# Node blocks in a turned order, a bank cleared and closed by one column, shorter bounds, and an eviction moved amid index copies

## The reference

```python
edge_index = stack([src, dst])
x = _layernorm(x + L0(x, node_type, edge_index, edge_type, ...))   # 3 relational convolutions, 5 relations
x = _layernorm(x + L1(x, ..., edge_index))                          # attention, edge score exp(-leaky_relu(s1[src] + s2[dst]))
x = _layernorm(x + L2(x, edge_index, edge_weight, ...))             # segment_sum(edge_weight * x[src], dst) @ W.T + b
x = _layernorm(x + L3(x, edge_index, edge_attr, ...))               # mean of edge_attr over dst, then a small MLP
```

## Time and profile before

| | before |
|---|---|
| median of 3 runs | 5267.58 us (5249.11 to 5267.61) |
| the profiled execution | 5260.04 us, span 5258.3 us |
| busy: PE, PEld | 3666.9 us (70%), 2929.5 us (56%) |
| busy: DVE, POOL, ACT | 2687.7 us (51%), 2380.1 us (45%), 1162.6 us (22%) |
| gathers of the three passes, line 608 | 2160, mean 1029 ns |
| visits (line 1130), blocks evicted (line 693) | 434, 385 |
| mean granted TensorE clock | 0.823 of full speed |
| chain that ended last | PE 36%, issue 20%, POOL 14%, DMA 13%, DVE 9% |

### The profile page before, as it was taken

How to read it: one execution, slowest core, us unless ns; L and a number is a source line. 1 busy time by engine, 2 the same in 40 slices (tenths; PEclk the granted TensorE clock), 3 DMA queues, 4 the chain that set the end, 5 groups by cost and what they waited for, 6 DMA issues and landing times.

```text
span 5258.3 us, 105311 instructions
## 1 busy us (share of the span) xinstructions
PE 3666.9 (70%) x20468; PEld 2929.5 (56%) x20688; DVE 2687.7 (51%) x6973; ACT 1162.6 (22%) x3868; POOL 2380.1 (45%) x2346
## 2 busy tenths in 40 slices
PE   4777566666777777766767677677777777584872
PEld 1233455555666666555555555566566666574862
DVE  7654344444444444355555555455554554794336
ACT  0122111111111122122222222223322322351112
POOL 0000233344455555466666666566666665002530
PEclk8999777787888888877777778788888888797986
DMA  2022222222333444322323233344444444255740
GB/s 75 33 63 68 73 61 67 74 73 81 97 101 115 121 120 123 108 76 78 86 80 84 81 90 89 105 115 117 126 124 123 129 125 115 104 208 150 203 133 13
DMA packets 478385, 526.90 MB, mean 100 GB/s; under 512 B 96596, under 2 KB 398238, under 8 KB 474670
## 3 DMA queue, kind: packets, MB, share of 16 engines
q1 hardware_dynamic: 252780, 246.52, 15.1%
q0 software_dynamic: 85824, 199.51, 14.0%
q10 hardware_dynamic: 139746, 80.46, 5.2%
HBM read 399.82 MB, written 126.39 MB: 100 GB/s over the span
## 4 chain that ended last, share of the span: by engine, by line
PE 36%; issue 20%; POOL 14%; DMA 13%; DVE 9%; DVEq 3%; ACT 2%; ACTq 1%; SPq 1%; POOLq 0%; another core or an unknown queue 0%
POOL msg_r L608 14%; DMA msg_r<-y_tab,idx_r 9%; PE psum L1566 9%; PE psum L1636 4%; PE psum L1568 2%; DMA msg_r<-x_tab,idx_r 2%; DVE shot_r L1136 2%; PE psum L1747 2%; PE psum L1709 1%; PE psum L1432 1%; PE psum L1494 1%; DVE h_t L1365 1%; PE psum L1748 1%; PE psum L1524 1%; PE psum L1506 1%
## 5 line engine op out<-in xcount | busy, mean ns | idle before, releaser
L608 POOL DMA_INDIRECT msg_r<-y_tab,idx_r x2160 | 2221.9, 1029 | 2223.9 <-issue 1161.6
L1566 PE MATMUL psum<-shot_r 128*128 128x200 f32 x2604 | 1000.1, 486 | 465.1 <-DVE shot_r L1136 437.3
L1130 DVE SCALAR_TENSOR_TENSOR shot_r<-edge_f,win_base,iota 128x600 bf16<-128x600 f32 x434 | 366.4, 844 | 1197.1 <-PE psum L1568 740.7
L684 ACT COPY idx_r<-row_i 128x1 int32 x2142 | 395.6, 190 | 2246.6 <-DMA msg_r<-y_tab,idx_r 2044.3
L1566 PEld LDWEIGHTS psum<-shot_r 128*128 128x128 f32 x2604 | 554.8, 262 | 476.5 <-issue 472.1
L1115 DVE TENSOR_SCALAR hot_r<-iota,edge_g 128x128 f32<-128x128 f32 x1602 | 454.4, 357 | 186.4 <-PE psum L1748 148.8
L1568 PEld LDWEIGHTS psum<-shot_r 128*100 128x100 bf16 x2604 | 444.7, 171 | 115.0
L1568 PE MATMUL psum<-shot_r 128*100 128x128 bf16 x2604 | 462.3, 271 | 0.0
L1747 PE MATMUL psum<-msg_r,shot_r 128*128 128x128 f32 x1440 | 338.1, 321 | 175.3 <-DMA msg_r<-y_tab,idx_r 94.6
L1636 PEld LDWEIGHTS psum<-hot_r,msg_r 128*128 128x128 f32 x2880 | 408.9, 218 | 16.7 <-DMA msg_r<-y_tab,idx_r 6.8
L1636 PE MATMUL psum<-hot_r,msg_r 128*128 128x128 f32 x2880 | 405.8, 300 | 11.3 <-DMA msg_r<-y_tab,idx_r 4.5
(11 more groups left out here) (322 smaller groups left out, 4932.6 us busy)
## 6 DMA issues: line engine op xcount, KB each, us to landing
msg_r<-in_attr SPq DMA_DIRECT2D x882, 64.0 KB
h_t<-count_tab SPq DMA_DIRECT2D x25, 1600.0 KB, 6.6
w_tab<-shot_r ACTq DMA_DIRECT2D x385, 100.0 KB
count_tab<-shot_r ACTq DMA_DIRECT2D x385, 100.0 KB
h_t<-w_tab SPq DMA_DIRECT2D x24, 1600.0 KB, 8.0
msg_r<-y_tab,idx_r POOLq DMA_INDIRECT x2160, 2.6
xn<-heavy_tab SPq DMA_DIRECT2D x76, 320.0 KB
y_tab<-y_s SPq DMA_DIRECT2D x25, 640.0 KB, 2.9
```

The source lines that it names most:

```text
L608: pool.indirect_dma_start(out=msg_r[:, q, 0:width], out_offset=None, in_=table, in_offset=bass.IndirectOffsetOnAxis(ap=idx_r[:, q:q + 1], ...
L684: nc.scalar.copy(idx_r[:, q:q + 1], of[:, q:q + COLS - U + 1][:, bass.ds(c0, 1)]).then_inc(s_idx[k], 1)
L1130: V.scalar_tensor_tensor(out=key_b, in0=of(KEY, KW), scalar=win_base[:, bass.ds(w, 1)], in1=to(KW), op0=ALU.subtract, op1=ALU.is_equal).th ...
L1566: T.matmul(win_ps, low_f[:, i, :], weighted_f[:, i, :], start=False, stop=False)
```

## The change

It has five parts.

1. **Turned order.** Position s of the running order now stands for block (s + 264) % 384 (`window_at`). `win_first` and `win_n`, from which `win_tab` is made, are copied from PSUM in two parts each so that they lie in that order. `win_base` and the rows of `w_tab` and `count_tab` go by the block's own number.
2. **One column.** `clear` and `close` of the block's bank write column 240 alone instead of 512 columns. Column 240 belongs to neither part.
3. **Bounds.** `window_of` takes a minimum and a maximum instead of remainders and quotients. `win_tab`'s second number is how many visits a block has.
4. **`window_at`** adds a remainder on VectorE and on ScalarE.
5. **Eviction amid the copies.** `one_group` calls `window_out_of_psum` behind the third `next_row` instead of the sixth.

```diff
+TURNED, SPARE = 264, 240
         def window_of(eng, x):
-            x = bounded(eng.snap((x + (AHEAD_OF - 1)) % AHEAD_OF), 0, PAST * NW, "it counts groups of the passes")
-            past = eng.snap((x // NW + (PAST - 1)) // PAST)
-            over = bounded(eng.snap((x + (AHEAD_OF - (NW - 1))) % AHEAD_OF * past), 0, PAST * NW, "it is how far x lies past the last window")
-            return x, over, bounded(eng.snap(x - over), 0, NW - 1, "the last window comes again where x is past it")
+            x = bounded(eng.snap(x - 1), 0, PAST * NW, "it counts groups of the passes")
+            slot = eng.alloc_register(name=f"slot{next(numbers)}")
+            eng.reg_alu(slot, x, NW - 1, op=ALU.min)
+            slot = eng.snap(slot, min_val=0, max_val=NW - 1)
+            over = eng.alloc_register(name=f"over{next(numbers)}")
+            eng.reg_alu(over, x, NW - 1, op=ALU.max)
+            over = eng.snap(over, min_val=NW - 1, max_val=PAST * NW)
+            return x, bounded(eng.snap(over - (NW - 1)), 0, PAST * NW, "it is at least the last window"), slot
...
-            at, over, w = x
-            v0, v1, c0, n_last = loaded(eng, win_tab[0:1, bass.ds(w, 1), :].rearrange("a b c -> a (b c)"),
-                                        most=(MOST, MOST, CHUNKS, CHUNKS))
-            return eng.snap(v0 + over * n_last), eng.snap(v1 + over * n_last), c0
+            at, over, slot = x
+            v0, n, c0, last = loaded(eng, win_tab[0:1, bass.ds(slot, 1), :].rearrange("a b c -> a (b c)"),
+                                     most=(MOST, CHUNKS, CHUNKS, CHUNKS))
+            v0 = eng.snap(v0 + over * last)
+            return v0, eng.snap(v0 + n), c0
+
+        def window_at(eng, slot):
+
+            return bounded(eng.snap((slot + TURNED) % NW), 0, NW - 1, "it is a remainder")
...
             def window_out_of_psum(x):
-                n, _, w = x
+                n, w = x[0], window_at(act, x[2])
...
                         next_row(k, of, c0, before16, q)
-                window_out_of_psum(x)
+                    if q == UH - 1:
+                        window_out_of_psum(x)
...
-            V.tensor_copy(win_first, psum[0:1, 4, 0:NW])
-            then(V.tensor_copy(win_n, psum[0:1, 5, 0:NW]))
+            for to, bank in ((win_first, 4), (win_n, 5)):
+                V.tensor_copy(to[:, 0:NW - TURNED], psum[0:1, bank, TURNED:NW])
+                last = V.tensor_copy(to[:, NW - TURNED:NW], psum[0:1, bank, 0:TURNED])
+            then(last)
...
-            V.tensor_scalar(out=win_tab[:, :, 1], in0=visited, scalar1=1.0, scalar2=None, op0=ALU.add)
+            V.tensor_copy(win_tab[:, :, 1], win_n)
...
             def window_hots(x):
-                w = x[2]
+                w = window_at(dve, x[2])
...
-                clear(psum[:, 2, :])
+                clear(psum[:, 2, SPARE:SPARE + 1])
...
-                close(psum[:, 2, :], s_wsum)
+                close(psum[:, 2, SPARE:SPARE + 1], s_wsum)
```

## The result

The changed kernel takes 5116.35 us, median of 4 runs (5114.44 to 5138.07), where the kernel before took 5258.34 in the same comparison (5244.24 to 5267.61). The ratio is 0.974, 95% interval [0.970, 0.978]: 142 us less, where 305 were forecast. The profiled execution has a span of 5112.8 us against 5258.3, and a mean granted clock of 0.823, as before.

What follows compares the result with a forecast made beforehand. No engine was taken as the bound but loops between engines: VectorE against TensorE in pass 0, through GpSimd in passes 1 and 2. Terms summed to -308 us from 5260.0, so 4952, stated as 4955, range 4850 to 5110.

Steps and rivals of the forecast that it cites:

- order, out of pass 0: Pass 0: 49 second visits leave it, at 6.3 us each, -309 us (bounds -296 to -328).
- order, into pass 1: Pass 1: the 49 second visits arrive, 43 at 4.0 us and six at 7, +214 us (+152 to +309).
- bounds, all passes: VectorE's register operations before a visit, in pass 0 and pass 1's dense stretch: 170 x 0.15, -26 us.
- one column and eviction, pass 0: Pass 0: a shorter close in the loop, -34 us, and an earlier eviction at 23 tile ends, -35 us.
- one column and eviction, pass 1: Pass 1 behind the dense stretch: no clear wait, shorter clear and close, 60 groups and 16 tile ends, -46 us.
- one column and eviction, pass 2: Pass 2: less waiting at the clear, shorter clear and close, 120 x 0.6, -72 us (0 to -163).
- the halving in passes 1 and 2: Passes 1 and 2: two periods share one delay of a half's buffers, so half the saving counts per group; -46, -72 us.
- The rival nearest to the measured time: All passes: ScalarE still stands before a landing or close when TensorE needs it; without 35 + 46 + 72, 5105 us; chance 0.05.
- The rival that a second visit costs in pass 1 what it cost in pass 0: Pass 1: single buffers there too, so +309 in place of +214 us, total 5050 us; chance 0.16.
- the rival's +213: TensorE's clock falls without the 512-column zeros, fast visits drop to 1.2 GHz: +213 us, total 5165; chance 0.08.
- The slower rival: Index copies become the bound as ScalarE waits for a close: 0.8 us in 360 groups, +288 us, total 5395; chance 0.04.
- the signs of being wrong: Pass 1 dense groups at 15 us, pass 2's clock below 0.8, or GpSimd waiting for the index copies (line 684).

Runs made afterwards that it cites:

- e1: The kernel before with the turned order alone (old bounds, 512-column clear and close, late eviction); ratio 0.988.
- e7: The kernel before with turned order and new bounds only, clear and close over 512 columns, eviction behind the sixth copy; ratio 0.969.
- e4: The changed kernel with clear and close over all 512 columns again, so order, bounds and moved eviction; ratio 0.969.
- e3: The changed kernel with the eviction back behind the sixth index copy, so order, bounds and one column; ratio 0.971.
- e9: e7 with the visits of passes 1 and 2 between the two halves of the sums, and VectorE making the first half's one-hots first; ratio 0.978.
- e8: The changed kernel with TensorE loading a block's bounds a second time, unused; ratio 0.976.
- e11: e10 with three more 512-column matmuls of zeros behind the clear in pass 0; 4986.7 us, ratio 0.948.
- e5: The changed kernel with the second half's one-hots of pass 2 on ScalarE moved ahead of the eviction; ratio 0.971.
- e10: A form for each pass: e7, but with pass 0's eviction amid the copies as in e4 and pass 1's visits between the halves as in e9; ratio 0.956.
- e15: The kernel of e10 run again, in a comparison where the kernel before took 5733 us; 5610.76 us, ratio 0.979.

## Why the prediction was wrong

The sign was right and the size was not: 142 us where 305 were forecast, and outside the range by 6 us. By its own steps, in spans, with the parts in the order e1, e7, changed:

| step | forecast | measured |
|---|---|---|
| order, out of pass 0 | -309 | -291 (e1) |
| order, into pass 1 | +214 | +223 (e1) |
| bounds, all passes | -26 (-60 to +17) | -91 (e7 less e1) |
| one column and eviction, pass 0 | -34 - 35 | -26 |
| one column and eviction, pass 1 | -46 | +23 |
| one column and eviction, pass 2 | -72 | +17 |
| sum | -308 | -145 |

163 us are missing. Passes 1 and 2 were to lose 118 us by one column and the eviction and grew by 40 instead: 158 us. Pass 0 is 43 short, the order 27. Against these stand 65 us that the bounds gave beyond their forecast. That the whole came as near as 142 is in part luck: with the forecast's bounds it would have been about 80.

**The failed step is the halving in passes 1 and 2** (-46 and -72 us): that half of what TensorE no longer waits for at the clear, and of what it saves at clear and close, comes off each group. The wait for ScalarE went as forecast, and the time didn't. The eviction alone (e7 to e4) made pass 1 20 us longer and pass 2 3, one column alone (e7 to e3) 18 and 20, both together 23 and 17. The wait before the clear had changed its name more than its size. In pass 1 it is, in e7:

```profile
PE psum L1445 <- ACT shot_r L704: 64.6, 66, 1.3
PE psum L1445 <- issue: 6.8, 12, 1.1
```

71.4 us, and 68.1 of "issue" in the changed kernel: ScalarE's eviction had run beside TensorE's own way from the last sum to the clear. What sets the length of a group there, and why an early eviction makes it longer, is not shown. 133.8 us of landing waits stand in the same groups (L1722, 125.4 in e7), which would fit a chain of gather, landing and sum that goes on when the clear is early; and e9 shows that 48 us can be had there by freeing three buffers ahead of the visits. The rival nearest to the measured time is the one that had 0.05, that the eviction's place brings nothing (5105): its gains of 46 and 72 us indeed didn't come. Its time is met by luck: the 65 us more from the bounds make up for 27 at the order, 8 in pass 0 and the 40 by which passes 1 and 2 grew. ScalarE did come to stand before the close (390.5 us of waits in pass 1 against 121.8 in e7).

**The order** was read rightly on both sides. 49 waits went, pass 0 has 10.1 us a group from its first third on, and the two dense groups of pass 1 shown above take 10.1 and 14.4 us, 12.3 in the mean, inside the forecast's 11.6 to 13.0. From 1833 to 2560 us it is 349 gathers, 58 groups, in 727 us, or 12.5 with the tile ends. The rival that a second visit costs in pass 1 what it cost in pass 0 is not borne out: 223, or 185 beside the other parts, against 291.

**The bounds** were mis-sized: 91 us where 26 were forecast. VectorE's part was about right. The 0.15 us stood for the new bounds and the remainder of `window_at` together, and against the 1.93 us before it is 1.76 in e7, or 0.17 less, and 1.84 in the changed kernel. That TensorE's part hides is not refuted in passes 0 and 1, where e8's second load of the bounds cost nothing. ScalarE's share had not been priced at all, nor had a gain in pass 2. How the other 65 us are shared is open.

**The clock** was the second step to fail. The forecast had it at nothing: it named the rival and set it aside with an argument: pass 2 runs at 0.85 with the same two 512-column matmuls a group as pass 1 with 0.78. That shows only that other work differs between the passes; it doesn't show what the fillers are worth in either. Taking them away moved the clock of pass 1 by 0.06 (e4 to the changed kernel 0.05) and of pass 2 by 0.04. The effect was far smaller than the rival's +213. The visits of pass 1 (line 1579) went from 433 us in e7 to 454 in e3, the sums from 287 to 336, and what reached the length was 3 to 18 us in pass 1 and 14 to 20 in pass 2. It doesn't account for the missing gains: e4 has the clock kept up and doesn't have them either. Forecast and rival were not exclusive, as their chances had it: part of one happened inside the other.

**The eviction's place** is half right. At pass 0's tile ends TensorE's wait for the table copy fell from 43.1 us (e7) to 15.4 (e4), and the pass by 25. But the same 25 come from one column alone (e3), where that wait is still 47.9, and both together give no more, 1275. That the two terms would add was wrong. What bounds pass 0 at 1275 beneath both was not tested; e11, which gets below it with a higher clock, points at TensorE's rate. In pass 2 the eviction also delayed what was queued behind it. The prediction had found 1.3 us to spare by GpSimd's need alone and had not asked when TensorE wants `plain_ones`: that wait rose from 27.2 to 152.9 us, though e5 shows that taking it away gives little. GpSimd's waits for its row numbers in pass 2 rose too, before and after:

```profile
POOL msg_r L608 <- PE psum L1748: 153.2, 77, 7.9
POOL msg_r L608 <- ACT idx_r L684: 36.7, 28, 2.4
```

```profile
POOL msg_r L618 <- PE psum L1761: 111.1, 68, 4.2
POOL msg_r L618 <- ACT idx_r L694: 80.9, 34, 7.4
```

GpSimd waited 42 us less for TensorE and 44 us more for ScalarE. The slower rival, index copies that become late, is there as a share of one pass, at a small part of its price.

**Of the marks set for it**, pass 0 was to take 1240 (1275), pass 1 1310 (1360), pass 2 1040 (1113), and a group behind the dense ones 8.0 (10.0, tile ends counted in). GpSimd's waits for TensorE in pass 2 were to halve (153.2 to 111.1). Of the signs of being wrong only one showed, GpSimd waiting for the index copies, and it had been there before (36.7 us in pass 2). TensorE's waits for line 694 of the kernel before vanished as said, and that is the lesson: the mark was met and the time wasn't.

A slip in its sums changes nothing: the bounds of its terms taken together reach from 4672 to 5290, not from 4690 to 5270.

## What to carry to other kernels

Where TensorE and another engine hand work to each other in turn, price a large matmul of zeros by two rows: its own time in the loop, and the busy time of the same matmuls behind it with and without it. An edit that only removes work from TensorE can bring nothing or lose a little, and zeros put into a wait that is there anyway can win. A wait that will vanish is worth nothing until the row of the next one in the same group has been read, whatever its sum.

## What the runs showed of the hardware that was not expected

- 511 columns less in each of two matmuls a group moved the granted clock of passes 1 and 2 by 0.04 to 0.06 and that of pass 0 not at all. In pass 1 it moved the middle one of 1440 sums from 275 to 421 ns and all of them together from 287 to 336 us (e7 to e3), for 18 us of the pass.
- Three 512-column matmuls of zeros a group in TensorE's idle time raised the clock of pass 0 from 0.89 to 0.94 and made it 50 us shorter. Where it was tried again, beside a kernel before of 5733 us, the whole was 37 us faster; three of one column did not do it (10 us of 5600, with overlapping runs).
- Register operations on bounds, which no profile counts as busy, were worth 91 us over 385 blocks and three engines (e1 to e7), 0.24 us for each block.
- The same kernel before took 5258 us in most comparisons and 5692 and 5733 in the last two, at a clock of 0.79 to 0.80; the cause is unknown. It isn't the chip alone: the comparison with e1 to e4 (5254) and the last one (5733) have the same chip number on record. e10 and e15 are one kernel in the two settings: up to the first gather both take some 558 us, and pass 0 then takes 1283 and 1413 us. The gain of e10 shrank from 4.4% to 2.1% there.
